# A state-space scan kernel: the store of the low dt rows is issued ahead of the replication of B

## The reference

```
x_norm = layernorm over the 96 channels
xz = x_norm @ W_in                      # 96 -> 2 x 192
xr = silu(causal conv of 4 taps over xz's first half)
dbl = xr @ W_xproj                      # -> 6 (dt rank) + 16 (B) + 16 (C)
dt = softplus(dbl[:6] @ W_dt + b_dt)    # 192 rows
h[d,n](t) = exp(dt[d] * A[d,n]) * h[d,n](t-1) + dt[d] * xr[d] * B[n]
y[d] = sum over n of h[d,n] * C[n] + xr[d] * D[d], times silu(z[d])
out = y @ W_out;  result = (forward + reversed) / 2 + input
```

## Time and profile before

| | |
|---|---|
| time, median of 3 runs | 5679.4 us (5677.27 to 5689.04) |
| the profiled execution's own time | 5688.73 us |
| its span | 5686.9 us |
| busy: TensorE, VectorE, ScalarE, GpSimd | 4461.4, 5250.7, 4314.0, 5083.4 us |
| mean granted clock of TensorE | 0.827 |
| traffic over the span | 954.66 MB, 168 GB/s |

### The profile page before, as it was taken

How to read it: one execution, slowest core, us unless ns; L and a number is a source line. 1 busy time by engine, 2 the same in 40 slices (tenths; PEclk the granted TensorE clock), 3 DMA queues, 4 the chain that set the end, 5 groups by cost and what they waited for, 6 DMA issues and landing times.

```text
span 5686.9 us, 47026 instructions
## 1 busy us (share of the span) xinstructions
PE 4461.4 (78%) x12946; PEld 1313.2 (23%) x12946; DVE 5250.7 (92%) x4449; ACT 4314.0 (76%) x6863; POOL 5083.4 (89%) x1737
## 2 busy tenths in 40 slices
PE   8877887778877888778887788777887778876676
PEld 3222222222222222222222222222222222221121
DVE  2799999999999999999999999999999999999998
ACT  3577777877787877878777777777777777777665
POOL 0599999999999999999899999999999999999998
PEclk7888888788887888788888888888888788887778
DMA  4576776777776776777777777776777677777776
GB/s 113 119 179 163 176 176 164 171 178 168 177 173 161 175 177 163 174 171 169 173 173 167 173 172 168 171 176 159 175 175 167 163 176 174 169 172 166 170 175 155
DMA packets 417567, 954.66 MB, mean 168 GB/s; under 512 B 56624, under 2 KB 56873, under 8 KB 382744
## 3 DMA queue, kind: packets, MB, share of 16 engines
q1 hardware_dynamic: 417304, 951.65, 70.8%
HBM read 770.08 MB, written 181.36 MB: 167 GB/s over the span
## 4 chain that ended last, share of the span: by engine, by line
DVE 22%; DMA 18%; POOL 18%; PE 16%; ACT 13%; issue 9%; SPq 4%; POOLq 0%; DVEq 0%; ACTq 0%
DVE X L1389 15%; POOL X L1497 12%; DMA bc_d<-bc 5%; POOL X L1486 5%; DVE X L1372 4%; PE ps L765 3%; PE ps L744 3%; ACT ps L1096 3%; DMA lo_d<-bc 3%; DMA out<-xf 3%; DMA hi_d<-S 3%; DMA lo<-lo_d 2%; PE ps L799 2%; DMA xf<-x_d 2%; ACT hid L982 1%
## 5 line engine op out<-in xcount | busy, mean ns | idle before, releaser
L1497 POOL TENSOR_TENSOR X<-X,cR 128x2048 f32<-128x2048 f32 x768 | 3473.6, 4527 | 64.3 <-ACT carry L1101 32.1
L1389 DVE TENSOR_TENSOR_SCAN X<-ps,carry,X 128x512 f32<-128x512 f32 x2688 | 3263.4, 1260 | 157.7 <-ACT ps L1096 157.6
L1096 ACT ACTIVATE ps<-hi,amat 128x512 f32<-128x512 f32 x2048 | 1376.0, 682 | 669.5 <-DVE X L1389 666.0
L799 PE MATMUL ps<-X,red 128*32 128x512 f32 x6144 | 912.4, 671 | 487.0 <-POOL X L1497 485.9
L1486 POOL TENSOR_TENSOR X<-lo,bR 128x2048 f32<-128x2048 f32 x258 | 1168.4, 4529 | 127.0 <-DMA lo<-lo_d 126.1
L1372 DVE TENSOR_TENSOR X<-hi,ps 128x2048 f32<-128x2048 f32 x512 | 1158.3, 2262 | 35.4 <-PE ps L799 30.1
L765 PE MATMUL ps<-win,w_u 97*128 97x512 f32 (+1 forms) x2080 | 1144.4, 702 | 3.4 <-ACT xr L1052 0.9
L1096 ACT ACTIVATE ps<-lo,amat 128x512 f32<-128x512 f32 x1026 | 691.1, 682 | 133.8 <-DVE X L1389 119.9
L780 PE MATMUL ps<-xr,wd 128*96 128x512 f32 (+1 forms) x520 | 433.4, 930 | 306.6 <-ACT xr L1052 249.6
L765 PEld LDWEIGHTS ps<-win,w_u 97*128 97x128 f32 (+1 forms) x2080 | 383.8, 195 | 682.9 <-issue 678.5
L1389 DVE TENSOR_TENSOR_SCAN X<-ps,X 128x512 f32<-128x512 f32 x384 | 445.3, 1202 | 34.5 <-ACT ps L1096 34.4
(11 more groups left out here) (125 smaller groups left out, 3842.1 us busy)
## 6 DMA issues: line engine op xcount, KB each, us to landing
hi<-hi_d SPq DMA_DIRECT2D x516, 512.0 KB, 8.0
bR<-bc_d SPq DMA_DIRECT2D x516, 256.0 KB, 4.6
lo<-lo_d SPq DMA_DIRECT2D x516, 256.0 KB, 4.6
cR<-bc_d SPq DMA_DIRECT2D x516, 256.0 KB, 7.2
hi_d<-S SPq DMA_DIRECT2D x258, 256.0 KB, 8.4
y_d<-yf SPq DMA_DIRECT2D x128, 256.0 KB, 10.2
yb<-y_d SPq DMA_DIRECT2D x112, 256.0 KB, 10.0
win<-xn_d SPq DMA_DIRECT2D x130, 195.1 KB
```

Source lines behind the costliest of these rows:

```text
L799: last = mm(p_y[GRP * j:GRP * j + GRP, :], red[:, :], X[:, slot(par, s), j, :], start=False, stop=(s in (LOW - 1, NB - 1)), skip_group_che ...
L1096: A_(p_a[i % RING][:, :], dt, ACT.Exp, scale=amat[:, column(i):column(i) + 1]).then_inc(s_exp, 1)
L1389: V.tensor_tensor_scan(h, a, h, 0.0 if head else carry[:, i:i + 1], ALU.mult, ALU.add).then_inc(s_scan, 1)
L1497: G.tensor_tensor(batch(par, s), batch(par, s), quads(cR, par, s), ALU.mult).then_inc(s_hc, 1)
```

## The change

In SyncE's body, `store_low(n + 1, nxt)` is moved three lines up: it is issued directly behind `store_bc`, ahead of `load_y(0)` (where there is one) and ahead of `load_b` with its wait for the landing of `bc_d`. With it move its own wait (for GpSimd's `times_x(1)`) and its two DMAs. The prologue keeps its order.

```diff
                 store_bc(n + 1, nxt)
+                store_low(n + 1, nxt)
                 if fin and rev:
                     load_y(0, (img + 1) * NCH, chunk_of(q, rev, odd), n * NB + (LOW + 2))
                 load_b(n + 1, nxt)
-                store_low(n + 1, nxt)
                 sp.wait_ge(s_exp, n * NT + LOW * BATCH)
                 load_low(n + 1, nxt)
```

## The result

The changed kernel took 5600.6 us (median of 4 runs, 5591.63 to 5608.77) against 5678.34 us for the kernel before beside it: a ratio of 0.9866 with a 95% interval of 0.9849 to 0.9883, 78 us faster by the medians and 76 us by the ratio, which is the figure used below. A later repetition on another chip gave 0.9848 (0.9835 to 0.9862). The forecast was 5646 us, 33 us faster. The direction was right, and so was the path named for the low rows. The size was less than half of what came, because about half of the gain came by a path that the sum had all but left out.

A forecast was written before the change was run, and what follows sets the result against it. VectorE and GpSimd, with the DRAM round trip for repeated rows, were taken to bound the kernel. 25 us for lo plus 8 us for the residual made 33 us, 0.58%, giving 5646 us; range 5600 to 5686 us.

The forecast's parts named there:

- What bounds the kernel: VectorE and GpSimd nearly always busy, DRAM round trip also on the chain; about 1 us of lo lateness became 1 us of VectorE.
- Cost of moving the store: SyncE before load_b: store_low's wait and 1.1 us of issues lie inside the bc_d wait; cost zero, cover 1.5 us.
- Rival C: SyncE before load_b locks to GpSimd's times_x(1): slower, 0.5 us in 64 forward bodies, 5711 us; chance 0.08.
- When load_low leaves: SyncE's load of low rows issues at T0+10.1 to T0+11.1 instead of T0+15.6, 4.5 to 5.5 us earlier.
- The sum: Chain waits for lo and the residual: 25 us plus 8 us, together 33 us, giving 5646 us.
- 20 x 1.24 us = 25 us: GpSimd's mean wait for lo vanishes in the 20 bodies where it lies on the chain: 25 us.
- 12 x 1.32 us = 16 us, of which half, 8 us: ScalarE's residual wait in 12 chain bodies, half counted because the residual still follows the window load: 8 us.
- A: GpSimd's waits for VectorE's scans take over the time won at lo: gain some 4 us, 5675 us; chance 0.18.
- B: All 64 forward bodies are on the path, each winning 1.24 us: 79 us, 5600 us; chance 0.12.
- D: lo_d, issued early, lands no earlier, so load_low leaves when it did: 5679 us; chance 0.06.
- load_y(0): Reversed bodies: this load moves behind the stores, from T0+0.4 to about T0+5 to T0+7; cost zero, cover 8 us.

The follow-up runs named there:

- partial splits: Changed kernel, load_high held to the 18th scan, window load cut 96+1 only in residual-loading bodies (0.9891) or only in the others (0.9883), 89+8 elsewhere.
- held kernels: Changed kernel with load_high held to the 18th scan (0.9935), or also load_c held to the 13th (0.9951), against the kernel before.

## Why the prediction was wrong

**What bounds the kernel: right, but not all of it.** The example's path (lo late, GpSimd, TensorE's sum, ScalarE's copy, VectorE) was the one. The forward bodies alone brought 60 of the 76 us, and ScalarE's waits for sums fell from 118.3 to 62.4 us. The bc_d transfer bounded it too: it had 5% of the chain, more than the two lo transfers had each, and the prediction took its landing as fixed.

**Cost of moving the store: nothing measurable came of it, but the reason given holds only in part.** I had the two issues and the wait for GpSimd inside the wait for bc_d. SyncE still waits for bc_d behind them in 87 of 129 bodies (103.3 us in all). In the others, the body above among them, bc_d has landed by then and store_low sets when load_b leaves: there the cover is gone. load_b is still earlier than it was, T0+6.8 against T0+8.1 on the mean. Rival C, SyncE locked to GpSimd, did not occur; the run with lo held late shows how such a lock looks, at 6018 us.

**When load_low leaves: the direction right, the distance too small.** I had T0+10.1 to T0+11.1; it was T0+8.0 in the body shown and T0+8.7 on the mean. lo_d lands 2.4 us after its issue at the median and not after the 4.9 I had carried over from its old place behind load_b. 96 rows and 1 row in place of 97 brought bc_d's landing from 8.0 to 1.6 us. With this the measurement agrees with the rule that I had drawn on. By the Trainium skill, page "DMA: Bandwidth & Descriptors", section "Why a DMA increments its semaphore by 16 and not by 1", a DMA uses the largest number of engines up to 16 that divides its row count, which is one for 97 rows and 16 for 96. The lo load itself then takes longer, 7.7 us instead of 4.6 us from issue to landing, with bR directly ahead of it, as I had reckoned. The high load won less than the C rows in front of it, 3.6 us against 6.9 on the mean, because hi_d landed after 11.6 us instead of 8.4.

**The sum: wrong, and this is the step that failed.** It had two terms. (The step of 5.5 us in it is a little long: load_low's last issue ends at 1640.74 and not near 1640.3. With 5.1 us the term would be 26 us instead of 25, which changes nothing.) The first, "20 x 1.24 us = 25 us" for lo, was measured with all else held late: 28 us. The second was "12 x 1.32 us = 16 us, of which half, 8 us" for all that comes from the earlier high load. It was mis-sized: with the high load held, 39 us of the 76 are gone. I had written that the high load "frees the queue for the next body's window, for the output store and the residual", and then priced only the residual, by its own share of the chain. I did not price the window load, which has no wait on the chain. But bc_d stands behind it on its engine. I had also read that the high load "ran until the next window load", as if the two did not meet.

Stretches of the two traces show that they do. Before, the window load left at 1659.29 and found the engines full with the high load (share 1.03). The share fell to 0.07, one engine's, only some 6 us later:

```profile
1659.40:1663.40 4.00, 4.00 (x13) 0.89 (x11) 4.00 (x4) 3.49 (x8) 3.92 (x2) 0.67 1.03 212
1663.40:1667.40 4.00, 3.74 (x14) 0.98 (x14) 4.00 (x6) 3.98 (x8) 4.00 (x2) 1.00 0.33 93
1667.40:1671.40 4.00, 2.80 (x13) 0.90 (x14) 4.00 (x3) 2.20 (x5) 4.00 (x3) 1.00 0.07 27
```

After, it left at 1640.43 into a nearly empty queue (0.20), and the long stretch on one engine began at once (0.05 to 0.09 in its first three microseconds, before other transfers join):

```profile
1636.40:1640.40 4.00, 3.70 (x5) 1.50 (x6) 4.00 (x5) 3.56 (x6) 3.92 (x3) 0.52 0.97 208
1640.40:1644.40 4.00, 4.00 (x13) 0.97 (x11) 4.00 (x4) 3.50 (x7) 4.00 (x2) 0.62 0.20 62
1644.40:1648.40 4.00, 4.00 (x18) 1.05 (x14) 4.00 (x6) 3.97 (x8) 4.00 (x1) 1.00 0.14 45
```

So a load_low issued early let SyncE issue the high load early. The high load was then out of the way when the next window load came. The window load's rows on their one engine were done sooner, and bc_d, the residual and the next lo landed sooner. The first term alone is a shift inside one body; the second is handed on.

The chain may have misled in one more way. It is one path; when two late things stand side by side, such as the residual and lo, it counts only one of them, so removing both could be worth more than the steps it shows. The partial splits (7 and 11 us apart, 27 together) point that way, but their uncertainty is as large as the effect: this is not shown.

**The rivals.** A (the wait is taken over) happened in part. In the changed kernel 35.3 of 113.5 us were waited again, most of it not at VectorE's scans as A has it but at ScalarE's carries. With only the low load early it was 60.6 of 86.7 us. A's price, a gain of 4 us, was far off. B (each forward body wins 1.24 us, 5600 us) had the forward bodies right, and its number by luck: it took all from lo, which alone brought 28 us. D: no.

**load_y(0): right.** Its delay cost nothing that can be measured.

What stays open: the 28, 9 and 39 us are differences between held kernels on several chips, each uncertain by 7 to 10 us, and the holds matched the old times only within half a microsecond on the mean, less well in single bodies. In the held kernels load_low itself leaves at T0+10.3, not T0+8.7, because bc_d lands late; so the 28 us are for a low load that is not quite as early as in the changed kernel.

## What to carry to other kernels

When a transfer is made earlier, follow everything behind it on the same queue into the next iteration, and price each thing that lands sooner, also those that nobody waits for directly but that stand in front of something awaited. A stretch of the profile in which the DMA share sits at one sixteenth while a small store takes 8 us to land points to a transfer on one engine; here it was a load of 97 rows, and cutting it into 96 and 1 removed the stretch's cost without any change of order. To value a wait, do not only count its steps on the chain, and add up the engine's other waits too, since part of what it no longer waits at one place it waits at the next. Hold the one thing late in an experiment, and watch that the hold is not tied to the work it delays.

## What the runs showed that I had not expected

A load of 97 rows of 2 KB held back four other transfers: bc_d, the residual, the piece `xp` (landing 9.5 us, 2.5 without it) and `yb` (10.0 and 5.6). Cutting one row off it took the residual's landing from 9.4 to 2.6 us and bc_d's from 8.0 to 1.6 us, and 1.4% off the time. And 89 rows in place of 97 on that engine were already worth some 18 us of 5680, give or take 11.
